# Attention layers of a graph network: own scores by groups of seven nodes, opening scores as weight columns

## The reference, cut to what matters

```python
def gat_conv(x, ei, W, a_src, a_dst, b, heads, out_ch):
    h = (x @ W).reshape(n, heads, out_ch)
    alpha_src = jnp.sum(h * a_src, axis=-1)
    alpha_dst = jnp.sum(h * a_dst, axis=-1)
    e = jax.nn.leaky_relu(alpha_src[src] + alpha_dst[dst], 0.2)
    m = jax.ops.segment_max(e, dst, num_segments=n)
    ex = jnp.exp(e - m[dst])
    s = jax.ops.segment_sum(ex, dst, num_segments=n)
    alpha = ex / (s[dst] + 1e-16)
    out = jax.ops.segment_sum(alpha[:, :, None] * h[src], dst, num_segments=n)
    return out.reshape(n, heads * out_ch) + b
```

## Time and profile before

| | |
|---|---|
| Time, median of 3 runs | 18843.47 us (18838.42 to 18850.27) |
| Span of the profiled execution, first to last instruction | 15220.1 us, 212898 instructions |
| Time of the profiled execution beside its span | not given on the page |
| PE busy, PEld busy | 7563.9 us (50%), 6275.1 us (41%) |
| DVE busy | 6961.0 us (46%) |
| ACT busy | 6200.7 us (41%) |
| POOL busy | 11256.0 us (74%) |
| Mean granted TensorE clock | 0.676 of full speed |
| HBM | 127 GB/s over the span |

### The profile page before, as it was taken

The page is one execution under the profiler, slowest core; times in us unless marked ns, Lnnn a source line. Parts: engine busy times, 40 slices in busy tenths (PEclk is TensorE's granted clock), DMA queues, the critical chain, the costliest instruction groups (busy, mean ns, idle before and its releaser), DMA issues. The chain is left out here.

```text
span 15220.1 us, 212898 instructions
## 1 busy us (share of the span) xinstructions
PE 7563.9 (50%) x51680; PEld 6275.1 (41%) x51680; DVE 6961.0 (46%) x24545; ACT 6200.7 (41%) x13834; POOL 11256.0 (74%) x11885
## 2 busy tenths in 40 slices
PE   5555552556564963444432444442344442766666
PEld 3444441555554862333332333332333332433334
DVE  6555554777775973333345333335222224433333
ACT  4777761677774842222221222221122222333333
POOL 5777776777776777777767777777777776777776
PEclk7777775887886965666655666665555555777777
DMA  5444442222222943444442444443333333333333
GB/s 186 162 162 162 163 152 73 96 93 92 91 93 84 347 157 119 147 148 148 147 127 87 147 148 148 148 147 68 82 85 85 85 85 71 108 119 119 119 119 93
DMA packets 939375, 1906.89 MB, mean 125 GB/s; under 512 B 438162, under 2 KB 517037, under 8 KB 898165
## 3 DMA queue, kind: packets, MB, share of 16 engines
q1 hardware_dynamic: 490085, 854.45, 17.0%
q0 software_dynamic: 356624, 523.18, 15.0%
q10 hardware_dynamic: 92240, 525.31, 8.7%
HBM read 1041.86 MB, written 889.14 MB: 127 GB/s over the span
## 5 line engine op out<-in xcount | busy, mean ns | idle before, releaser
L113 POOL DMA_INDIRECT eg_got<-gat_table,edge_rows x4983 | 4706.1, 944 | 1533.4 <-issue 1502.9
L113 POOL DMA_INDIRECT e_got<-table,edge_rows x3322 | 3142.3, 946 | 1044.2 <-issue 998.6
L1624 PE MATMUL eg_ps_sum<-eg_got,eg_equal 128*128 128x136 f32 (+1 forms) x9984 | 2219.0, 402 | 0.0
L1624 PEld LDWEIGHTS eg_ps_sum<-eg_got,eg_equal 128*128 128x128 f32 x9984 | 2114.7, 310 | 30.2 <-issue 1.3
L1639 ACT ACTIVATE eg_outs<-eg_ps_sum 128x544 f32<-128x544 f32 (+1 forms) x1248 | 683.9, 548 | 3397.3 <-PE eg_ps_sum L1624 3395.7
L118 POOL DMA_INDIRECT sorted_rows<-sort_rows,sort_dest x1661 | 1612.1, 971 | 506.3 <-issue 506.3
L1688 DVE COPY eg_own<-eg_got 128x128 f32<-128x128 f32 (+1 forms) x312 | 68.6, 220 | 3420.2 <-DMA eg_got<-gat_table,edge_rows 3420.2
L1669 PE MATMUL eg_up<-ident,eg_own 128*128 128x128 f32 (+1 forms) x312 | 137.4, 440 | 2567.9 <-DVE eg_own L1688 2567.9
L1669 PEld LDWEIGHTS eg_up<-ident,eg_own 128*128 128x128 f32 (+1 forms) x312 | 47.3, 152 | 2650.5 <-issue 2537.5
L1718 ACT ACTIVATE eg_equal<-eg_equal_b 128x512 f32<-128x512 bf16 x1248 | 782.4, 627 | 482.5 <-issue 482.5
L686 PE MATMUL e_ps_sum<-e_got,e_equal 128*128 128x64 f32 x3328 | 567.5, 329 | 686.7 <-DMA e_got<-table,edge_rows 686.5
(11 more groups left out here) (510 smaller groups left out, 20397.0 us busy)
## 6 DMA issues: line engine op xcount, KB each, us to landing
gat_out<-eg_outs ACTq DMA_DIRECT2D x208, 1152.0 KB
eg_equal_b<-equal_d SPq DMA_DIRECT2D x312, 512.0 KB
out<-e_outs ACTq DMA_DIRECT2D x104, 1024.0 KB
values<-e_zeros_b SPq DMA_DIRECT2D x104, 768.0 KB
values_q<-e_zeros_b SPq DMA_DIRECT2D x104, 768.0 KB
sort_value<-values_q SPq DMA_DIRECT2D x104, 768.0 KB
e_value<-values SPq DMA_DIRECT2D x104, 768.0 KB
eg_got<-gat_table,edge_rows POOLq DMA_INDIRECT x4983
```

The source lines that it names most:

```text
L113: return e.indirect_dma_start(out, None, table, bass.IndirectOffsetOnAxis(ap=index, axis=0), **kw)
L1624: last_i = e.matmul(ps_sum[q % 2][:, i, 0:FG], equal[q % 4][:, i, :], got[k][:, t, :], start=True, stop=True)
```

## The change

It has five parts.

1. **Own scores by groups of seven nodes.** `values2` gets rows of 56 scores (7 nodes by 8 heads). For a span of seven neighbouring nodes one row is written, at the first edge of the span's first node: 14 scatters in place of 98. In the pass, PE turns seven planes of values in two parts (four, then three, through one PSUM tile), DVE carries each on along edges of the same span with a scan, picks the plane by the node's place in its span and sums the seven. The span of an edge is found by a multiplication and a rounding. Tile values are gathered by span too. A small table stage (`GroupTables`) makes the rows of the spans in the stage after the second layer.
2. **Opening scores as weight columns.** The products of the weights with the two score vectors are summed on DVE once per layer and stand as extra columns of the weights (FO = HF + 2 heads columns). PE makes all in one product; ACT, no longer DVE, copies the result out, and a copy on ACT regroups the own scores by spans.
3. **Shares in small factors.** Closing makes exp of both sides in one ACT instruction, works the denominator into the two small factors, and then has two long multiplications and a sum, and the bias. The ELU is a Relu and an Exp on ACT and one DVE instruction.
4. **Unchecked collects.** The tables have one more row behind (zeros, and for attention a lowest maximum), written in the first pass; nodes without edges point to it. The collects have no bound and no clearing.
5. **In the first pass**, more tables and one more load in their chain, and clears seven times as large for `values2`.

The diff, cut to its core:

```diff
+SPAN = 7
+SPANS = NT // SPAN
+VALUES = SPAN * HEADS
+NEUTRAL = EP + T
-        self.values2 = self.dram("values2", (EP, HEADS))
+        self.values2 = self.dram("values2", (EP, VALUES))
...
+            e.dma_start(self.group_start[:, :], group_tab.rearrange("(p g n) -> p g n", p=P, n=SPAN)[:, :, 0]).then_inc(tables_in, 16)
             e.dma_start(self.end_plain[:, :], to_nodes(plain_tab)).then_inc(tables_in, 16)
...
+        def dve_own_scores(e, it, new):
+            k_t = key_t[new % 2]
+            e.tensor_scalar(quotient[0:W, :], k_t[0:W, :], 1.0 / SPAN, -(SPAN // 2) / SPAN, ALU.mult, ALU.add).then_inc(grouped.sem, 1)
+            e.tensor_scalar(quotient[0:W, :], quotient[0:W, :], ROUND, -ROUND, ALU.add, ALU.add).then_inc(grouped.sem, 1)
+            e.tensor_tensor(kin[0:W, 1:P], quotient[0:W, 1:P], quotient[0:W, 0:P - 1], ALU.is_equal).then_inc(grouped.sem, 1)
+            e.scalar_tensor_tensor(of_group[0:W, :], quotient[0:W, :], -float(SPAN), k_t[0:W, :], ALU.mult, ALU.add).then_inc(grouped.sem, 1)
+            dve_fill(e, it, new, early)
+            dve_fill(e, it, new, late)
+            for i in range(SPAN):
+                last_i = e.scalar_tensor_tensor(chosen[0:W, i, :], of_group[0:W, :], float(i), fill[0:W, i, :], ALU.is_equal, ALU.mult)
+            e.reduce_sum(ends_score[new % 2][0:W, :], chosen[0:W, :, :].rearrange("p n e -> p e n"), axis=AX.X).then_inc(spread.sem, 1)
...
-                e.tensor_tensor_scan(ends_score[new % 2][0:W, :], ln[0:W, :], up[new % 2][0:W, 1, :], 0.0, ALU.mult, ALU.add).then_inc(spread.sem, 1)
+                dve_own_scores(e, it, new)
...
 class Collect:
-            e.wait_ge(self.cleared, (j + 1) * len(self.parts))
             for t in range(ts.start, ts.stop):
-                gather(e, self.to[:, t, :], self.out[:, :], self.end_row[:, t:t + 1], self.out.shape[0] - 1).then_inc(self.rows_in[j], 16)
+                gather(e, self.to[:, t, :], self.out[:, :], self.end_row[:, t:t + 1]).then_inc(self.rows_in[j], 16)
+class SpreadGroups:
+            done(e, j)
+            for t in range(ts.start, ts.stop, SPAN):
+                g = t // SPAN
+                scatter(e, self.values[:, :], self.group_row[:, g:g + 1], self.rows[:, g, :, :].rearrange("p h n -> p (h n)"), EP - 1).then_inc(self.starts_out, 16)
...
 GatOpen, was vector(), now scalar()
-            e.tensor_copy(hid[:, :, 0:HF], ps[:, :, self.kept_at:]).then_inc(out, 1)
-            e.tensor_tensor(s_prod, h, across(self.a_src[:, :], k), ALU.mult).then_inc(out, 1)
-            e.reduce_sum(hid[:, :, HF:FG], by_head(s_prod, heads), axis=AX.X).then_inc(out, 1)
-            e.tensor_tensor(d_prod, h, across(self.a_dst[:, :], k), ALU.mult).then_inc(out, 1)
-            e.reduce_sum(self.dst[:, ts, 0:heads], by_head(d_prod, heads), axis=AX.X).then_inc(out, 1)
+            e.activation(self.hid(j)[:, at, :], ps[:, :, 0:FG], ACT.Copy).then_inc(out, 1)
+            e.activation(dst_rows[:, at, :], ps[:, :, FG:FO], ACT.Copy).then_inc(out, 1)
```

More of the change, by code:

```diff
@@ L154, in nodes, with spans, spans_of, by_span @@
     return table.rearrange("(p t) c -> p t c", t=NT)
+def spans(table):
+    return table.rearrange("(p g) c -> p g c", g=SPANS)
+def spans_of(ts):
+    return slice(ts.start // SPAN, ts.stop // SPAN)
+def by_span(a):
+    return a.rearrange("p (g n) h -> p g n h", n=SPAN)
 def by_group(table):
@@ L1671, in pe_stage @@
             sums(2)
+            if new is not None:
+                values_up(e, it, new, late)
             if mid is not None:
@@ L1891, in vector @@
         def vector(e):
-            for made in (message, masked, spread, added):
+            for made in (message, masked, spread, added, filled):
                 e.sem_inc(made.sem, made.ahead)
@@ L2582, in block0 @@
         self.sort()
-        out = self.dram("out0", (EP + T, D))
+        out = self.sums[0]
         last = self.dram("last0", (2, T, D))
@@ L2693, in block1 @@
         values = self.values1
-        out, last = self.dram("out1", (EP + T, D)), self.dram("last1", (2, T, D))
+        out, last = self.sums[1], self.dram("last1", (2, T, D))
         self.carried_pass(values, out, last)
@@ L2715, in gpsimd @@
             collect.gpsimd(e)
+            groups.ready(e)
             opened.gpsimd(e)
@@ L2729, in vector @@
         def vector(e):
-            opened.clear(e)
-            collect.vector(e)
-            for j in range(n_chunks + 1):
-                if j < n_chunks:
-                    lin2.vector(e, j, join)
-                if j:
-                    opened.vector(e, j - 1)
-                if j < n_chunks:
-                    norm.vector(e, j)
+            groups.vector(e)
+            opened.fold(e)
+            for j in range(n_chunks):
+                lin2.vector(e, j, join)
+                norm.vector(e, j)
         def scalar(e):
@@ L2744, in scalar @@
                 if j:
-                    opened.lin.scalar(e, j - 1)
+                    opened.scalar(e, j - 1)
                 if j < n_chunks:
@@ L2788, in vector @@
         def vector(e):
[L2789 to L2799 removed]
+            opened.fold(e)
+            for j in range(n_chunks):
+                close.vector(e, j)
+                elu.vector(e, self.feat[:, CHUNKS[j], 0:HF], close.part[:, :, :])
+                e.sem_inc(closed, 1)
         def scalar(e):
```

329 lines of the change are left out of this document (212 added, 117 removed).

## The result

The changed kernel takes 18723.1 us (median of 4 runs, 18673.8 to 18737.4), the kernel before beside it 18841.8 us: a ratio of 0.9931, with a 95% interval of 0.9916 to 0.9945. That is 119 us less. Forecast were 313 us less, 18530 us, with a range from 18380 to 18650: the direction is right, the time is outside the range.

A forecast was written before the change was run, and what follows sets the result against it. POOL's gathers were taken to bound the passes, and POOL's work to end the two closing stages. Savings 62 + 116 + 114 + 12 + 7 + 7 less 5 made 313 us: 18843 to 18530 us, range 18380 to 18650.

The forecast's parts named there:

- Between the passes: Stages outside the attention passes: fewer scatters, shorter closing and opening, unchecked collects save 62, 116, 114, 12, 7 and 7 us.
- The first pass, at +5: First pass: larger clears cost nothing, but a longer chain of tables and one more load add 5 us (3 to 9).
- The signs named beforehand: Profile signs: passes of 2105 to 2110 us, 14 scatters per stage, collects at 944 ns, stages about 230, 217, 215 us.
- POOL's loss beside DVE's long instructions: First closing: gathers lost 33 us beside six long DVE instructions per chunk; with five, 29 us.
- The passes at nothing: Attention passes: DVE's new 8.3 us per group fits its 10.6 us idle under POOL's 20.0 us, so no cost.
- No row shows where the other 3623 us go. I take them to be the same before and after.: Whole kernel: timed median 18843.5 us against profiled span 15220.1; the difference was taken as unchanged.
- a gain of the runs that differs from that of the span: Sign that would prove the forecast wrong, concerning the 3623 us between profiled span and timed runs.
- The third closing at -12 us: After the third attention layer: no check, no memset wait, less contention and a shorter last closing save 12 us.
- DVE's piece is longer: Rival, attention passes: DVE's new piece exceeds its idle time, a group takes 20.5 us, 18686 us; 7%.
- Stretched time: Rival, whole kernel: unprofiled time lies along POOL's work, each profiled microsecond worth 1.24, gain 388 us, 18455 us; 22%.
- Opening on ACT: Rival, stages between passes: ACT's ordered queue becomes the bound, 27 us per chunk in place of 21.8, 18625 us; 14%.
- Contention in the passes: Rival, attention passes: nine new two-input DVE instructions slow POOL's gathers by 1.4 us per group, 430 us, 18960 us; 5%.

The follow-up runs named there:

- a_split: Changed kernel with the late scans, choices and sum of own scores put behind DVE's multiplication of the rows; 18859.4 us against 18992.4, ratio 0.9935.
- a_double: Changed kernel with every sum matmul of the attention passes done twice; 19355.6 us, slow pace.
- b_double: Kernel before with every sum matmul of the attention passes done twice; 19510.4 us, slow pace.
- b_same2: Kernel before, unchanged, profiled once more on another chip; 15219.4 us (span 15217.7), quick pace.
- b_fewer: Kernel before with only every seventh of the 98 own-score scatters of each opening; 18840.9 us where the kernel before takes 18992.4.
- a_same: Changed kernel, unchanged, run beside its variants on a third chip; 14919.0 us where the kernel before took 15218 and 15248.
- a_same2: Changed kernel, unchanged, profiled again on another chip; 14926.4 us (span 14930.7), quick pace.
- a_dve2: Changed kernel with the check back in the third layer's collects, all seven turnings, but two of seven scans and choices; 14929.9 us, quick pace.

## Why the prediction was wrong

By its own steps, where "quick" is the pair of spans 15217.7 and 14930.7:

- **Between the passes.** For the stage after the second layer, the first, second and third closing, the last stage and the one after the first layer, -62, -116, -114, -12, -7 and -7 us were forecast. Quick: -61, -111, -106, -11, -6 and -7. At the slow pace (a_split and a_double against b_double, same chip) -77, -117, -111, +47, -1 and +2 to +4. The two closings that carry the forecast hold at both paces. The first pass, at +5, took 1.4 us more at the quick pace. In sum the quick pace gave 287 and 294 us for the 313 forecast. The signs named beforehand: 14 scatters per stage, a median of 945 ns for unchecked collects, stages of 230, 217 and 215 us; it is 229, 218 and 219.
- **POOL's loss beside DVE's long instructions** was to fall by a sixth with one of six gone. The collects of the first closing have a mean of 1294 ns at the quick pace, 349 above their median, where the earlier trace rows have 337 above: it did not fall. In the trace 30 collects are long, one beside each of the five long instructions of six chunks, as the prediction counted; but each loses 1.14 us, where before the change 37 long collects (b_same2) lost 0.90 us each, nine of them beside instructions with one input that the prediction did not count. The Trainium skill's rule (SBUF — State Buffer, "Who interferes with whom"), by which a DVE instruction with two SBUF inputs holds up a GpSimd instruction that reads SBUF, agrees on which collects are held, as all five have two such inputs. The missing fall is 4 us of the stage.

```profile
L119 POOL DMA_INDIRECT g1c_agg<-shares,end_row x98 | 126.8, 1294 | 63.3 <-POOLq L112 33.7 <-issue 29.5
```

- **The passes at nothing.** Quick: +6, +7 and -1 us. DVE's wait for rows fell from 11.0 us per group (3421.2/312 in b_same2) to 6.2, so the new piece took 4.8 us of the cover, less than the 8.3 it was put at: 1.6 us more came from DVE's wait ahead of the multiplication of the rows, which fell from 513.9 to 7.9 us in all. Its sum over 896 values takes 1662 ns, not 1090. The cover held. At the slow pace the cover for which the piece was reckoned is not there: the kernel before already takes 23.9 us per group, and DVE hardly waits for rows (95.6 us in all in b_fewer). Most of the piece finds another one, DVE's wait ahead of the multiplication, in b_fewer 6.9 us per group (the two lines below over 312) and in the changed kernel at this pace 7.2 us in all three passes together:

```profile
DVE eg_got L1712 <- ACT eg_outs L1739: 1217.6, 202, 12.0
DVE eg_got L1712 <- issue: 949.6, 110, 41.6
```

  The passes still grow by 127 us in a_split against b_fewer; 0.41 us per group hang on five sevenths of the piece.
- **"No row shows where the other 3623 us go. I take them to be the same before and after."** This is the step that failed. They were not outside the profile: they lie in the passes, the sort and some stages, in an execution of another pace than the timed ones. From b_same2 to b_fewer the sort grows by 1169 us, each attention pass by some 380, the first pass by 472 and the last by 736. And they were not the same for both kernels: the changed one takes 3797 us more at the slow pace (18723.1 against 14926.4). The condition under which the cover was computed, POOL at 20.0 us per group, did not hold in the runs that count. The sentence under the signs ("a gain of the runs that differs from that of the span") named the test, and runs 24% above the span should have lowered the chance of every step that rests on slack.
- **The third closing at -12 us** was +47 at the slow pace: no rival had it.

Slow pace, summed: -77 - 117 - 111 + 47 - 1 + 2 + 127 = -130 us, and a_split was measured 133 below the kernel before. For the changed kernel itself the stages alone give -261 with its own profile against b_double's, and -119 was measured, so 142 us lie in the passes and around. Of the 194 us between the forecast and the result these 142 and the 58 of the third closing stage (+46 for -12) are more than all; the other stages give a little more than forecast.

**The rivals.** "DVE's piece is longer" (7%, 20.5 us per group, 18686 us) is the nearest, with the right place and about the right price, 0.4 to 0.5 us per group; its reason, the piece against idle time at POOL's pace, is not what happened. "Stretched time" (22%) is wrong where it was to apply: the closing stages, 218 us, are not stretched at all, and the gain shrank rather than grew. "Opening on ACT" (14%): at the quick pace the stage after the second layer is 229 us as forecast; at the slow pace it is 323, but with three waits of TensorE, 84.6 us, that end with nothing that the profile shows, ahead of the opening:

```profile
PE b1c_lin_ps_o L3129 <- issue: 84.6, 3, 42.1
```

The kernel before has 400 us there, so the gain stays. "Contention in the passes" (5%): the gathers of these passes have a mean of 949 ns at the quick pace, for 944, and of 955 at the slow one, for 948 in b_fewer: 0.1 us per group, less than a tenth of the 1.4 us of that rival. The longest single one takes 1125 ns, 1119 before the change. The Trainium skill's rule (SBUF — State Buffer, "Who interferes with whom") makes no exception for short instructions; if they do contend here, their price is small.

## What to carry to other kernels

Hold a profiled execution's own time against the timed runs before anything else: with 24% between them its slack is not theirs, while stages in which POOL runs through almost without waiting carried over (the two closings gave 106 to 117 us at either pace, 116 and 114 were forecast). Work put under cover is safe only as long as the engine that covers it sets the pace; name the ring that takes over if another is slowed, and what each microsecond in it costs. And a cheaper instruction can still lose: leaving out the check saves 52 ns per collect and cost 48 us in one stage at the slow pace.

## What the runs showed of the hardware

- **Two paces.** The kernel before takes 15.22 to 15.25 ms on four chips and 18.84 to 18.99 on three. At the slow pace two closing stages of the changed kernel are as long as at the quick one, the stage after the second layer is 41% longer (323 us for 229) and the passes 19%, with the same busy time; the sort is 54% longer (3264 us for 2118), and there PE's busy time grows too, 1664 us for 1207, at a granted clock of 0.66 for 0.80. Why is open; no run here changes it.
- **What the stands look like.** They are late updates of semaphores. In the attention group shown, DVE goes on 6.9 us after the end of TensorE's turning by its record, 0.1 us at the quick pace, and within 0.03 us of the semaphore's update; and DVE takes steps 1.40 us apart, mostly where it waits for its own semaphore of the step before, in the third closing, 32 times in the result's profile, never in that stage of a_same. The seven slow traces also record only 80 to 92 thousand semaphore updates, the thirteen quick ones 268 to 271 thousand. Whether missing records and late updates have one cause is open.
- **Unchecked collects.** On chips of the slow pace they go with these steps of DVE in the third closing, not in the first, the second or the last stage, whose collects are unchecked too (218, 219 and 208 us, as with checked ones or less). While these collects run, the slow traces record 2.1 to 2.3 semaphore updates per us in that stage without the check and 10 to 11 with it, the quick ones 15 to 16 either way (b_same2, a_same2). What is special there was not found.
- **TensorE's or DVE's work.** Which of the two counts in the slow passes is open too: the run for it (a_dve2) was of the quick pace.
